# Head-pair loop of a cross-attention stage: scores placed right behind another pair's value product, output product one pair later

## The reference, cut to what matters

```
kvx = jnp.einsum('bsi,oi->bso', cond, w_kv_x)          # cond: (8, 1601, 512)
kx, vx = jnp.split(kvx, 2, axis=-1)
kx = _ln(kx.reshape(b, sc, g, d), kxln_w, kxln_b)      # g = 8, d = 128
vx = vx.reshape(b, sc, g, d)
xout = _gqa(qx, kx, vx).reshape(b, s, nh * d)          # 16 query heads, two for each g

def _gqa(q, k, v):
    scores = jnp.einsum('bsghd,btgd->bghst', q, k) * scale
    p = jax.nn.softmax(scores, axis=-1)
    return jnp.einsum('bghst,btgd->bsghd', p, v)
```

## Time and profile before

| | |
|---|---|
| median of 3 executions | 2839.76 us (2838.6 to 2843.26) |
| the profiled execution, own time | 2842.95 us |
| its span in the trace | 2841.1 us |
| PE busy with matmuls | 2658.2 us, 94% of the span |
| PEld busy | 2204.3 us, 78% |
| DVE busy | 1881.8 us, 66% |
| ACT busy | 1577.8 us, 56% |
| POOL busy | 471.0 us, 17% |
| the head-pair loops | 8 stretches between about 300 and 1820 us |

### The profile page before, as it was taken

The page is one execution under the profiler, slowest core; times in us unless marked ns, Lnnn a source line. Parts: engine busy times, 40 slices in busy tenths (PEclk is TensorE's granted clock), DMA queues, the critical chain, the costliest instruction groups (busy, mean ns, idle before and its releaser), DMA issues.

```text
span 2841.1 us, 39319 instructions
## 1 busy us (share of the span) xinstructions
PE 2658.2 (94%) x13638; PEld 2204.3 (78%) x13638; DVE 1881.8 (66%) x4789; ACT 1577.8 (56%) x2967; POOL 471.0 (17%) x392
## 2 busy tenths in 40 slices
PE   6889999999999999999999999989988788959999
PEld 5778787887887887887878878768766677747887
DVE  6847648547557466476485477668578685558997
ACT  6945436436345345354364364446665666837776
POOL 3402002002011011020020020033332322011111
PEclk9989999999999999999999999999999989979999
DMA  3432022021031030130220211636665622529996
GB/s 122 134 118 86 10 57 87 15 79 60 19 99 36 24 109 22 39 97 10 57 72 15 79 50 56 215 86 166 183 170 164 156 54 83 180 90 396 372 374 232
DMA packets 255060, 317.83 MB, mean 112 GB/s; under 512 B 128648, under 2 KB 166152, under 8 KB 241680
## 3 DMA queue, kind: packets, MB, share of 16 engines
q1 hardware_dynamic: 252064, 311.05, 34.6%
q0 software_dynamic: 2800, 4.27, 0.6%
HBM read 274.16 MB, written 46.98 MB: 113 GB/s over the span
## 4 chain that ended last, share of the span: by engine, by line
PE 75%; DVE 11%; ACT 6%; issue 3%; DMA 3%; SPq 2%; POOL 1%; POOLq 0%; DVEq 0%; ACTq 0%
PE ps L103 20%; PE ps L105 20%; PE ps L104 20%; PE ps L818 3%; PE ps L774 2%; PE ps L846 2%; DVE lnw L2066 1%; PE ps L799 1%; DVE zz L2069 1%; DVE cv L2033 1%; PE ps L839 1%; DMA ca<-cat_d 1%; ACT gb L1818 1%; SPq L1729 1%; PE ps L524 1%
## 5 line engine op out<-in xcount | busy, mean ns | idle before, releaser
L1188 POOL TENSOR_TENSOR lnw<-lnw,half 128x8 f32<-128x8 f32 x88 | 144.4, 1640 | 1217.7 <-DVE lnw L908 1217.7
L103 PE MATMUL ps<-whf,cth 128*128 128x512 f32 (+1 forms) x832 | 336.5, 404 | 2.0 <-ACT kn L1061 2.0
L103 PE MATMUL ps<-cnh,pth 128*128 128x512 f32 (+1 forms) x832 | 330.0, 397 | 6.4 <-issue 6.4
L105 PE MATMUL ps<-whf,ctl 128*128 128x512 f32 (+1 forms) x832 | 326.4, 392 | 0.0
L104 PE MATMUL ps<-wlf,cth 128*128 128x512 f32 (+1 forms) x832 | 325.3, 391 | 0.0
L104 PE MATMUL ps<-cnl,pth 128*128 128x512 f32 (+1 forms) x832 | 324.9, 391 | 0.0
L105 PE MATMUL ps<-cnh,ptl 128*128 128x512 f32 (+1 forms) x832 | 324.6, 390 | 0.0
L2507 DVE TENSOR_TENSOR ml<-mr,mh 128x2048 fp32r<-128x2048 f32 x90 | 203.4, 2288 | 32.5 <-ACT mh L2451 32.5
L1099 ACT ACTIVATE pr<-ps,sm 128x1601 f32<-128x1601 f32 x56 | 89.6, 1600 | 206.1 <-DVE sm L961 206.1
L980 DVE TENSOR_TENSOR ptl<-ps,pth 128x512 fp32r<-128x512 f32 (+1 forms) x256 | 139.1, 585 | 78.8 <-ACT pth L1111 78.4
L1124 ACT ACTIVATE xo<-ps 128x128 f32<-128x128 f32 x64 | 17.7, 277 | 311.9 <-PE ps L846 311.9
(11 more groups left out here) (340 smaller groups left out, 6419.1 us busy)
## 6 DMA issues: line engine op xcount, KB each, us to landing
mr<-in_moe SPq DMA_DIRECT2D x90, 1024.0 KB, 6.7
ctr<-in_ctxt SPq DMA_DIRECT2D x96, 256.0 KB, 3.0
pr<-in_ctxn SPq DMA_DIRECT2D x96, 256.0 KB
wv<-in_wv SPq DMA_DIRECT2D x64, 256.0 KB, 2.8
wr<-in_wqkv SPq DMA_DIRECT2D x64, 256.0 KB, 2.9
wvf<-in_wattn SPq DMA_DIRECT2D x12, 1024.0 KB, 4.9
ca<-cat_d SPq DMA_DIRECT2D x16, 512.0 KB, 4.1
qk_d<-cv SPq DMA_DIRECT2D x32, 256.0 KB, 3.3
```

The lines of the kernel that those rows point to most:

```text
L103: pe.matmul(dst, lh, rh, start=first, stop=False)
L105: return pe.matmul(dst, ll, rh, start=False, stop=last)
L1188: po.tensor_tensor(rs[0:w, s, :], nv[0:w, s, :], half[0:w, 0:8], ALU.pow).then_inc(kx_rs, 1)
```

## The change

Three queues are reordered; no instruction is added or removed. On PE the scores of pair g + 2 stand right behind the values of g (the scores of pair 1 stay between the two halves of the turning in pair 0). The output product of m - 2 stands between turn groups 0, 1 and 2, 3 of pair m, from g = 2 on, and that of pair 6 at the end of the batch. The output product of pair 7 stays where it was, in the next batch or stage. On DVE the low parts of groups 2 and 3 come ahead of the reciprocal. On ACT the exponential of g + 1 comes behind the high parts of groups 2 and 3 and behind `pcT`, and the output copy moves with its product.

```
         s3_pe
                 for g in range(8):
                     m = 8 * b + g
                     p_turn_pe(pe, b, g, (0, 1))
-                    if g + 1 < 8:
+                    if g == 0:
                         for w in range(4):
-                            score_pe(pe, b, g + 1, w)
+                            score_pe(pe, b, 1, w)
+                    elif g >= 2:
+                        xo_pe(pe, m - 2)
                     p_turn_pe(pe, b, g, (2, 3))
...
                         pc_turn_pe(pe, m - 1)
                     pv_pe(pe, b, g)
-                    if g > 0:
-                        xo_pe(pe, m - 1)
+                    if g + 2 < 8:
+                        for w in range(4):
+                            score_pe(pe, b, g + 2, w)
+                xo_pe(pe, 8 * b + 6)
         s3_dv
                     if g + 1 < 8:
                         softmax_dv(dv, b, g + 1)
+                    p_low_dv(dv, b, g, (2, 3))
+                    if g + 1 < 8:
                         t_rinv[g + 1] = rinv_dv(dv, b, g + 1)
-                    p_low_dv(dv, b, g, (2, 3))
                     if g + 2 < 8:
                         kq_low_dv(dv, m + 2)
         s3_ac
+                    if g >= 2:
+                        xo_ac(ac, m - 2)
+                    p_high_ac(ac, b, g, (2, 3))
+                    if g > 0:
+                        pcT_ac(ac, m - 1)
                     if g + 1 < 8:
                         p_exp_ac(ac, b, g + 1)
-                    p_high_ac(ac, b, g, (2, 3))
                     if g + 2 < 8:
                         kq_high_ac(ac, m + 2)
-                    if g > 0:
-                        pcT_ac(ac, m - 1)
...
-                    if g > 0:
-                        xo_ac(ac, m - 1)
+                xo_ac(ac, 8 * b + 6)
```

## The result

The changed kernel takes 2859.96 us (median of 6, 2856.78 to 2866.43), the kernel before 2842.01 us beside it (median of 6). The ratio is 1.0067, with a 95% interval from 1.0054 to 1.0080: 15 to 23 us slower. The medians themselves are 18.0 us apart. The forecast was 2862. The profiled execution took 2859.57 us, with a span of 2857.8.

What follows compares the result with a forecast made beforehand. PE was taken to set the pace (busy 1480.07 of 1500 us); uncovered gaps and seams add 2.76 us a batch, 22.1 over eight batches, to the 2839.76 us median, giving 2862, range 2849 to 2874.

Steps and rivals of the forecast that it cites:

- The cover of the turning: Between the turning's halves, pairs 1 to 7: without scores, PE's work (2.28 or 1.39 us) is under ACT and DVE's 2.77.
- x: Time from a pair's first transpose to the turn of the result, forecast at 2.77 us in pairs 1 to 7.
- The sum: One batch from pair 1 through pair 7's output product: 97.24 us before, 100.00 after, 2.76 more; 22.1 for the kernel.
- The seams: Block borders on PE: scores behind values 0.09 us cheaper (2.33), first transposes behind scores 0.06 dearer in six pairs.
- The median: Whole kernel: the median before, 2839.76 us, plus 22.1 gives 2861.9, say 2862.
- How the gap splits: PE's new gaps between the turning's halves: 1.38 us in pair 1, 0.49 in pairs 2 to 6; pair 7's shrinks to 0.49.
- output product is cover enough: Rival, chance 0.08: in pairs 2 to 7 only PE's work of 2.28 us counts; no change, 2838 us.
- The recorded waits: L818's waits for `ptl`: up to 56; 0.98 us in pair 1, about 0.1 in pairs 2 to 7, 13 in all.
- DVE's and ACT's reordering: Vector queues: `kql` ends 9.8 us after the first transpose, the values at 12.1; margin 2.3 us, cost nothing.
- SP's queue: Output store and `wv` load follow the copy ending at 2.16 us; next batch's context loads 1.7 later, cost nothing.
- The clock: Rival, chance 0.04: gaps in each pair bring slow-pace matmuls behind every turning, 67 us more, near 2930.

Runs made afterwards that it cites:

- two widths in the gap: Changed kernel, but two widths of the scores (w = 2 and 3) wait for the next pair's gap, behind the output product; 2834.71 us, ratio 0.9979 to before.
- short low parts: Changed kernel, PE untouched; DVE leaves out low parts of three of four blocks of groups 0 and 1, except in the first pair; 2838.69 us, ratio 0.9998 to before.
- scores-alone kernel: Changed kernel with the output product and its ACT copy moved back behind the values; 2903.82 us, ratio 1.0226 to before.
- last width in the gap: Changed kernel, but the last width of the scores (three 66-column matmuls) waits for the next pair's gap, behind the output product; 2847.23 us, ratio 1.0027 to before.

## Why the prediction was right, point by point

*The cover of the turning.* Right, and shown from three sides: by taking the rest of the cover away (56 recorded waits of 0.98, +64 us), by giving it back in two doses, and by shortening DVE's part without touching PE. x stayed where ACT and DVE put it, 2.77 in pair 7 and 2.82 in the middle pairs (2.77 and the 0.06 that I had for the seam behind scores).

*The sum.* A middle pair was to take 14.50 us and takes 14.48 to 14.52. The batch was to be 2.76 us longer and is 2.72. By the stage's own blocks the loss is 21.8 us, against the 22.1 of the prediction.

*The seams.* Right in size. The scores take 316.12 - 313.78 = 2.34 us behind values (2.33 was forecast), and x behind scores is 2.83 where it is 2.77 behind values. But the 0.06 belongs to the narrow matmuls at the end of the scores, 66 columns wide, and not to scores as such: where the last width was moved away, so that 512-column matmuls come last, x is 2.77 or 2.78 in the middle pairs too.

*The median.* It moved by 18.0 us, with an interval of 15 to 23, where 22.1 was forecast. That the forecast of 2862 lies only 2 us from the measured 2859.96 is in part luck: the base of 2839.76 was 2.25 us under the median of six, and the loss came out 4 us smaller than the sum, which partly cancel. In the profiled executions, the time from the last turn of a result to the end of the span is 2857.8 - 1832.35 = 1025.45 us after and 2841.1 - 1810.15 = 1030.95 before, 5.5 less, in code that the change doesn't touch:

```profile
1832.35 0.60 PE L839 MATMUL ps<-cst,pc 128*128 128x128 f32 x4
```

Over all ten profiled kernels this remainder lies between 1025.45 and 1031.79 us with no order by what was changed in the stage ahead: the two widths in the gap have the longest. Before and after, PE starts 4643 matmuls in it at a granted clock of 0.95; its busy time differs by 1.1 us and its idle time by 4.4, so it is mostly waits of PE in those later stages. I take it for variation between executions, of up to 6 us; that is argued and not shown, and what makes these waits differ stays open.

*How the gap splits.* Here a term was mis-sized, without a consequence for the sum. I gave PE 2.28 us of work in x for pairs 2 to 6, and 0.06 for the seam apart from it, and so a gap of 0.49. The short low parts show that the work is 2.44 there, 0.10 more than 2.34: the eight transposes of groups 0 and 1 take longer ahead of the product (0.87 behind values, in the last pair above) than ahead of scores (0.79). The gap is 2.82 - 2.44 = 0.38. As x is set by the chain and not by the work, the pair's time didn't move. But the rival "output product is cover enough" and the forecast for the short low parts, both reckoned with 2.28, come out too low by 0.10 x 40 pairs = 4 us, and 1 us more for pair 7.

*The recorded waits.* My forecast of the recorded waits was wrong: 13 us in all with small waits in pairs 2 to 7; in PE's rows there were 7.8 us in 8 waits, one a batch, since the recorded ends of the product's matmuls cover the rest. In PEld's rows the waits are there in all 56 pairs, as forecast for L818: 112 of them, 32.9 us, 21.6 more than before.

*DVE's and ACT's reordering.* Right: nothing within 0.2% when done alone. In the changed kernel the exponential starts 4.56 us after the first transpose (forecast 4.6), and `kql` ends at 9.78 (9.8), 2.4 us ahead of the scores.

*SP's queue.* In pair 7 of batch 0 the next batch's first context load (L458) is issued 3.20 us after the first transpose, and 1.44 before: 1.8 later, where 1.7 was forecast. No cost of it is left to find: gaps and seams alone were to make 2.76 us a batch, and 2.72 are measured.

*The clock.* It stayed at 1.00 in the stage, even in the scores-alone kernel, whose halves of the turning have nothing between them in 56 pairs. But I had misread the trace of before when I wrote that the 1.2 GHz pace comes only behind long idle. Its windows from 57 to 60 us show a granted clock of 0.50 behind a recorded idle of 2.28 us:

```profile
56.69 3.59 PE L406 MATMUL ps<-cst,qn 128*128 128x128 f32 x16 [2.28 <-ACT qn L332]
```

At 193.2 us the clock falls to 0.50 where the last recorded idle of PE, ended at 192.28, is 1.69 us long. So the idle that came before a fall was far shorter than the 10.35 us I went by, and the rival was nearer than I wrote; that it didn't come true is shown by the clock of 1.00 alone. The row also bears on transposes: the 16 at 56.69 were PE's only work from the idle until 60.02, and from 60.1 us on the granted clock was 1.00.

*The rule that groups should rotate so that one's evacuation overlaps the next one's matmuls* (the Trainium skill, "Perfetto Trace Analysis", "Matmuls") agrees with all of it: 2.42 us of scores covered the evacuation, 0.89 of product didn't.

## What to carry to other kernels

Between a step that fills a bank and the next use of that bank, what counts is how much other work the queue holds, not whose it is: measure the evacuation chain from a place where nothing covers it, and leave at least that much there. A block that is moved out of such a place should leave enough behind to cover the chain (here 1.84 us were enough where 2.42 had stood, and 1.14 and 0.89 were not), and short leftovers (an output product, the next loop's first matmuls) are best put where the cover is missing, here in the last pair, not where it is ample.

Read pipelined matmuls from start to start, and look at the waits of their loads as well: PE's row of recorded waits was the same before and after (7.8 us, 8 times) and the kernel 0.7% slower, while PEld's went from 17 waits to 112. Here PEld's sum even comes near the gaps: 0.38 us in 48 pairs and 1.38 in 8 make 29 us, and 32.9 are recorded.

## What was not expected of the hardware

A block of transposes costs differently by its neighbours: the same eight take 0.79 us between the product and scores, 0.87 between values and the product (401.71 - 400.84), 0.92 between scores and the product (331.56 - 330.64), and 0.88 there when the scores end in 512 columns and not in 66 (345.06 - 344.18, the last width in the gap). Five of them take 0.60 behind scores and 0.62 behind the product when nothing holds them, and 0.76 when the last waits for its bank.
